# Causal blocks without the one above the diagonal: three columns of 64 queries per head in place of four, 64x64 products, a second load of x

## The reference, cut to what matters

```
q = layernorm(x);  k = v = ctx
ig, fg = gates(q, k, v)                       # one value per head and row
cs = cumsum(log_sigmoid(fg))
log_D = where(t <= s, cs[s] - cs[t], -inf) + ig[t]
D = exp(log_D - max over t);  C = (q k^T / 8) * D
h = C / (max(|sum C|, exp(-max)) + eps) @ v;  per-head layernorm * out_w
x = x + h;  x = x + fp8_gemm(layernorm(x)) + bias
```

## Time and profile before

| | us |
|---|---|
| median of 3 runs | 2239.78 (2235.75 to 2244.46) |
| the profiled execution | 2241.11 |
| its span, first to last instruction | 2239.0 |
| TensorE busy | 2020.9 (90%) |
| VectorE busy | 1865.2 (83%) |
| ScalarE busy | 1464.7 (65%) |
| GpSimd busy | 818.4 (37%) |
| mean granted clock of TensorE, as a share of full speed | 0.962 |

### The profile page before, as it was taken

One profiled execution on the slowest core, in us unless ns is written; L12 is line 12 of the kernel. 1 busy time (PEld: TensorE's weight loads), 2 busy tenths in 40 slices (PEclk: granted clock), 3 DMA queues, 4 the chain that ended last, 5 costly groups with the idle time before them and its releaser, 6 DMA issues. The chain is left out here.

```text
span 2239.0 us, 70236 instructions
## 1 busy us (share of the span) xinstructions
PE 2020.9 (90%) x26252; PEld 1445.6 (65%) x26252; DVE 1865.2 (83%) x4380; ACT 1464.7 (65%) x3137; POOL 818.4 (37%) x659
## 2 busy tenths in 40 slices
PE   2899999989999899998989999899998999989986
PEld 1666666666666666676666666666666766766763
DVE  5699987979889797897989979798887988979986
ACT  2677776757667576675767767576675766757753
POOL 0234343424334333433433433343343333434343
PEclk9999998989999999999999999999999999999998
DMA  5133323322323232232223233234232332332311
GB/s 164 23 112 94 108 94 96 98 87 87 114 87 103 71 115 87 87 114 87 87 88 114 87 101 101 87 86 115 87 97 77 115 87 87 114 87 87 105 39 38
DMA packets 206898, 207.82 MB, mean 93 GB/s; under 512 B 8848, under 2 KB 140816, under 8 KB 206496
## 3 DMA queue, kind: packets, MB, share of 16 engines
q1 hardware_dynamic: 206496, 202.59, 29.9%
HBM read 135.45 MB, written 67.11 MB: 90 GB/s over the span
## 5 line engine op out<-in xcount | busy, mean ns | idle before, releaser
L1082 POOL TENSOR_TENSOR x<-x,w_out 128x512 f32<-128x512 f32 x256 | 369.8, 1465 | 1078.3 <-DVE x L884 1078.3
L820 DVE TENSOR_TENSOR dec<-qk,dec 128x1024 f32<-128x1024 f32 x256 | 312.9, 1222 | 139.8 <-PE qk L420 88.5
L555 ACT ACTIVATE dec<-arg 128x512 f32<-128x512 f32 x512 | 301.3, 588 | 158.4 <-PE arg L406 158.3
L420 PE MATMUL qk<-qT,kT 64*128 64x128 f32 x4096 | 304.7, 290 | 71.4 <-issue 39.7
L1086 POOL TENSOR_TENSOR x<-x,x_sb 128x512 f32<-128x512 f32 x256 | 321.5, 1277 | 0.0
L420 PEld LDWEIGHTS qk<-qT,kT 64*128 64x128 f32 x4096 | 260.1, 195 | 85.9 <-issue 41.6
L445 PE MATMUL work<-c_sb,dec 128*64 128x65 f32 x8192 | 307.6, 230 | 1.3 <-DVE carry L828 1.3
L669 ACT ACTIVATE zq<-y,s_inv 128x1024 fp8e4<-128x1024 bf16 x128 | 142.5, 1114 | 229.3 <-PE y L466 229.3
L445 PEld LDWEIGHTS work<-c_sb,dec 128*64 128x64 f32 x8192 | 272.9, 143 | 29.1 <-issue 2.7
L481 PE MATMUL y<-w_ffn,zq 128*128 128x512 bf16 x1024 | 276.6, 394 | 0.0
L1074 POOL TENSOR_TENSOR k_w<-c_sb,facs 128x512 f32<-128x512 f32 x128 | 133.9, 1046 | 326.5 <-ACT facs L621 325.1
(11 more groups left out here) (108 smaller groups left out, 3362.4 us busy)
## 6 DMA issues: line engine op xcount, KB each, us to landing
x_sb<-in_x SPq DMA_DIRECT2D x128, 512.0 KB, 4.1
c_sb<-in_ctx SPq DMA_DIRECT2D x256, 256.0 KB, 5.4
out<-o_sb SPq DMA_DIRECT2D x128, 512.0 KB, 5.1
w_ffn<-in_L_ffn_kernel SPq DMA_DIRECT2D x1, 512.0 KB
w_out<-in_L_xattn_out_w SPq DMA_DIRECT2D x1, 256.0 KB
gsel<-in_c_gsel SPq DMA_DIRECT2D x1, 128.0 KB
b_ffn<-in_L_ffn_bias SPq DMA_DIRECT2D x1, 128.0 KB
ident<-in_c_ident SPq DMA_DIRECT2D x1, 64.0 KB
```

Source lines behind the costliest of these rows:

```text
L420: last = mm(qk_ps[:, u, c * P:(c + 1) * P], kT[half, r, c, t * P:(t + 1) * P], qT[half, r, c, t * P:(t + 1) * P], start=True, stop=True)
L555: af(dec[:, q, :], arg_ps, ACT.Exp).then_inc(decays[q].sem, 1)
L820: tt(dec[:, U * t:U * t + U, :], qk_ps[:, :, :], dec[:, U * t:U * t + U, :], ALU.mult).then_inc(weighted[t].sem, 1)
L1082: pl.tensor_tensor(h, h, w_out[:, :], ALU.mult).then_inc(h_scaled[t].sem, 1)
```

## The change

**The blocks.** Of a tile's 128x128 block of a head, the quarter with late keys and early queries is above the diagonal. The change works in quarters of 64x64. The lower half of the partitions (0 to 63) holds the first 64 keys of a tile, the upper half the last 64, and a head's three columns of 64 queries hold, for both tiles: the first keys of tile 0 by its first and second queries and the first keys of tile 1 by the second queries; above them the last keys in the same way (tile 1's keys stand with their halves exchanged). A head now takes 192 columns for both tiles in place of 256. `scores(b, p)` makes a pair of head pairs for both tiles, and `within` sums the first keys with `c_first`, a copy of the first 64 rows of each tile that is loaded extra, and the last ones with `c_sb`.

**TensorE.** `scores` goes from 8 products of 128x128 per call to 16 of 64 keys by 128 or 64 queries; `across` from 8 products of 128 queries to 16 of 64; `arg` from 6 matmuls over 512 or 128 columns to 14 over 256, 128 or 64 columns with 64 output partitions each; `scan_rows` from 4 to 16 on four column strips. Where a matmul reads 64 partitions and writes 64, it uses a quarter of the array.

**x and the output.** `x_sb` shrinks to 4 batches; x is loaded a second time for the residual, into `o_sb` itself (now two buffers), where `finish` later writes the output. So that load must wait for the store of two batches before.

**The order.** All five `slot` functions are written anew. Decays are double-buffered.

```diff
             def load_x(b):
-                r = b.k % RING
-                if b.follows(RING):
-                    sp.wait_ge(*x1_set[1].of(b - RING))
+                r = b.k % X_RING
+                if b.follows(X_RING):
+                    sp.wait_ge(*q_normed.of(b - X_RING))
                 sp.dma_start(x_sb[:, r, :, :], rows_of(x, b)).then_inc(x_in[r], 16)
+
+            def load_own(b):
+                if b.follows(2):
+                    sp.wait_ge(stored, b.count(16, -16))
+                sp.dma_start(o_sb[:, b.k % 2, :, :], rows_of(x, b)).then_inc(own_in[b.k % 2], 16)
...
+            def load_first(b):
+                r = b.k % 2
+                if b.follows(2):
+                    sp.wait_ge(*summed[1].of(b - 2))
...
             def arg(b, q):
...
-                mm(arg_ps, ident_bf[:, :], later[:, :].unsqueeze(1).broadcast_to([P, 4, P]),
-                   start=True, stop=False)
-                mm(arg_ps, tops[:, t * P:(t + 1) * P], hsel[:, row:row + NH - 1:2].unsqueeze(2).broadcast_to([P, 4, P]),
-                   start=False, stop=False)
-                for h in range(4):
...
+                mm(low[:, :, 0:2, :], tops[:, 0:Q], two, start=True, stop=False)
+                mm(high[:, :, 0::2, :], tops[:, 2 * Q:3 * Q], two, start=True, stop=False)
+                mm(low[:, :, 2, :], tops[:, 3 * Q:4 * Q], one, start=False, stop=False)
+                mm(high[:, :, 1, :], tops[:, Q:2 * Q], one, start=False, stop=False)
+                for h in range(2):
+                    neg = hsel_neg[:, row + U * h:row + U * h + 1].broadcast_to([P, Q])
+                    mm(low[:, h, 0:2, :], neg, tops[:, S:S + 2 * Q], start=False, stop=False)
+                    mm(high[:, h, 0::2, :], neg, tops[:, S + 2 * Q:S + 4 * Q], start=False, stop=False)
+                    mm(low[:, h, 2, :], neg, tops[:, S + 3 * Q:S + 4 * Q], start=False, stop=False)
+                    mm(high[:, h, 1, :], neg, tops[:, S + Q:S + 2 * Q], start=False, stop=False)
...
+                for i in range(2):
+                    c = 2 * p + i
+                    out = qk_ps[:, :, i * HEAD:(i + 1) * HEAD].rearrange("p u (s n) -> p u s n", s=3)
+                    for lower, key, query, n, to in ((True, 0, 0, 2, slice(0, 2)), (False, 3, 2, 2, slice(0, 3, 2)),
+                                                     (True, 2, 3, 1, slice(2, 3)), (False, 1, 1, 1, slice(1, 2))):
+                        for u in range(U):
...
             def across(b):
...
+                    for rows in (slice(0, P // 2), slice(P // 2, P)):
+                        for u in range(U):
...
-                if b.follows(1):
-                    act.wait_ge(*summed[q // U].of(b - 1))
-                af(dec[:, q, :], arg_ps, ACT.Exp).then_inc(decays[q].sem, 1)
+                if b.follows(2):
+                    act.wait_ge(*summed[1].of(b - 2))
+                af(dec[:, b.k % 2, q, :], arg_ps[:, 0:U * HEAD], ACT.Exp).then_inc(decays[q].sem, 1)
...
+                tt(mine, qk_ps[:, :, 0:U * HEAD], mine, ALU.mult).then_inc(weighted[p].sem, 1)
...
-                if t == 0 and b.follows(1):
-                    dve.wait_ge(stored, b.count(16, 0))
...
             def residual(b, t):
                 pool.wait_ge(*h_scaled[t].of(b))
-                pl.tensor_tensor(x1[:, b.k % 2, t, :], x1[:, b.k % 2, t, :], x_sb[:, b.k % RING, t, :],
+                if t == 0:
+                    pool.wait_ge(own_in[b.k % 2], b.count(16, 16, 2))
+                pl.tensor_tensor(x1[:, b.k % 2, t, :], x1[:, b.k % 2, t, :], o_sb[:, b.k % 2, t, :],
```

More of the change, by code:

```diff
@@ L316, in slot @@
             def slot(m):
[L317 to L322, removed]
+                if live(m + 5):
+                    load_c(m + 5)
+                if live(m - 3):
+                    load_own(m - 3)
+                if live(m - 2):
+                    load_first(m - 2)
+                if live(m - 4):
+                    store(m - 4)
+                if live(m + 7):
+                    load_x(m + 7)
             slots(sp, slot)
@@ L435, in within @@
             def within(b, t):
-                pe.wait_ge(*weighted[t].of(b))
+                r = b.k % RING
+                for p in range(2):
+                    pe.wait_ge(*weighted[p].of(b))
                 if t:
@@ L440, in within @@
                     pe.wait_ge(*state_kept.of(b))
+                    pe.wait_ge(first_in[b.k % 2], b.count(32, 32, 2))
                 for u in range(U):
[L442 to L447, removed]
+                    for c in range(C):
+                        at = c % 2 * HEAD
+                        heads_dec = dec[:, b.k % 2, c // 2 * U + u, at:at + HEAD]
+                        cols = slice(u * W, (u + 1) * W)
+                        for rows, slot, src in ((slice(0, Q), 0, c_first[:, b.k % 2, t, c, cols]),
+                                                (slice(Q, P), 1 + t, c_sb[:, r, t, c, cols])):
+                            last = mm(work_ps[rows, u, c * W:(c + 1) * W], heads_dec[:, slot * Q:(slot + 1) * Q], src,
+                                      start=True, stop=True)
                 last.then_inc(summed[t].sem, 1)
@@ L452, in across @@
                 pe.wait_ge(*state_kept.of(b))
+                pe.sem_inc(pe_passed, 1)
                 for c in range(C):
[L454 to L457, removed]
+                    for rows in (slice(0, P // 2), slice(P // 2, P)):
+                        for u in range(U):
+                            half = slice(DH * u, DH * u + DH)
+                            last = mm(work_ps[rows, u, c * W:(c + 1) * W],
+                                      qT[half, b.k % RING, c, P + rows.start:P + rows.stop],
+                                      state[half, c, :], start=True, stop=True)
                 last.then_inc(crossed.sem, 1)
@@ L741, in _ @@
             setup(ve.memset(n_eps[:, :], EPS))
+            for t in range(T):
+                for r in range(2):
+                    setup(ve.memset(c_first[t * Q:(t + 1) * Q, r, t, :, 0:U * W:U * W - 1], 1.0))
             setup(ve.memset(ln_qs[:, :], math.log(Q_SCALE)))
```

360 lines of the change are left out of this document (190 added, 170 removed).

## The result

The changed kernel takes 2402.62 us (median of 4 runs, 2387.95 to 2405.53) against 2238.33 (2235.75 to 2244.46) for the one before in the same comparison: ratio 1.0713, 95% interval 1.0688 to 1.0738. It is slower by 7%; 2117 was forecast, with a range of 2010 to 2225.

The account below looks back on a forecast made before the run. The DMA loop was to replace TensorE as bound: 86.4 + 5 of filling and setup, 127 plain slots at 13.7, 31 scan extras at 5.0, 14 loop starts at 7.5 and 25.3 give 2116.6, forecast 2117; range 2010 to 2225.

Parts of the forecast that it names:

- What bounds the kernel: Before the change, TensorE bounds a plain slot at 14.41; scans add 5.35 per four slots, a loop start 9.5.
- TensorE and VectorE, part by part: Plain slot after the change: TensorE falls from 14.41 to 13.1, VectorE from 12.74 to 12.2.
- The new loop through the DMA queue: From store through own load, residual, statistics and finish to the next store: 13.7 a plain slot, replacing TensorE as bound.
- Own lands 8.7 after the store's issue (8.3 to 9.1): In the DMA loop, the second load of x lands 8.7 after the issue of the store in that slot.
- The clock: Rival: TensorE idling in scan slots lowers its clock; scans cost 8 and loop starts 14, 2301 in all; 5 in 100.
- 8.7 + 1.4 + 3.4 + 0.2 = 13.7: DMA loop in a plain slot: own's landing, residual with handover, VectorE to the end of finish, then the store's issue.
- Where the loop starts again: At each restart of the eight-slot loop, TensorE's and VectorE's standings overlap: 7.5 instead of 9.5, between 6 and 10.
- The DMA loop is late: Rival: five transfers a slot in one queue make a plain slot 14.3, 2193 in all; 20 in 100.
- own landing more than 10 behind the store: Sign in the DMA loop that would show the forecast wrong: own landing more than 10 after the store's issue.

Follow-up runs that it names:

- the fast version: Changed kernel with the second load of x in its own buffer one slot earlier and the first rows of ctx one slot earlier: 2078.71 us, ratio 0.9278.
- The changed order: Changed kernel with the second load of x and the first rows of ctx issued ahead of ctx's three pieces in SyncE's slot: 2202.79 us, ratio 0.9832.
- The table of four kernels: Changed kernel 2402.62 us; first rows of ctx a slot earlier 2362.25; own buffer for the second x, a slot earlier, 2341.12; both 2078.71.

## Why the prediction was wrong

**What bounds the kernel.** Right once the new waits are gone. The fast version is the forecast without them: forecast 13.1 for TensorE, 5.0 for the scans, 7.5 a start; measured 13.23, 5.8 (17.60 + 14.62 - 2 x 13.23, for undisturbed slots), and, from its first `keep_heads` at 90.7 to its last at 2044.5, (1953.8 - 127 x 13.23 - 31 x 5.8) / 14 = 6.7. The scans lie above their range of 4.5 to 5.35. The 25.3 behind the last `keep_heads` in the sum is 1.0 more than its rows give (24.3), which changes nothing.

**TensorE and VectorE, part by part.** Right within 0.1 a term: the quadrants run four at once, a change of shape costs 0.12 to 0.15, the score product 0.952. The Trainium skill (TensorEngine Tiling, Key Properties) says that a change of the tiling mode drains TensorE, and these rows agree that it costs something; that did not help, since the bound had left TensorE.

**The step that failed is "The new loop through the DMA queue": "Own lands 8.7 after the store's issue (8.3 to 9.1)".** In batches 16 to 111 it landed 10.9 behind it in the median, 9.3 to 11.4 in the middle 8 of 10. My 8.7 was a piece of ctx of before, issued 2.0 behind the first transfer and landing 5.4 later, plus 1.3 for 512 KB. Own was issued 3.8 behind the store, not 2.0, and took 7.0 from there, not 6.7: the issue is the term that I had too small. Two things hold it. Four issues (x and three pieces of ctx) stand between the store's and that of own, and the store must have landed, which takes 3.3; I had named this wait and given it no time. The changed order tells them apart. There own is issued 3.2 behind the store, 0.02 after the store's landing, and takes 5.6 to its own, which gives 8.9. So of the 2.0 gained the issues ahead of own are 0.6 and the transfers of ctx ahead of it 1.4; the wait for the store stays. With 10.9 for 8.7 the sum comes to 15.9 of the 17.0 measured.

**The second loop had no price.** "The extra load of ctx's first rows queues behind own and is needed by the first `within` at about the same time" was one sentence, where it was a loop of its own: `load_first` waits for `summed[1]` of two batches before and is issued last of all behind the store; it landed 11.8 behind it in the slot shown. From there `within`, scores, `across` and `carried` lead to `finish` and the next store. The table of four kernels shows that it alone holds the kernel at 2341.

**The clock.** The forecast had the idle only in the scan slots. In the changed kernel TensorE now waits for `c_first` in 107 of the 128 batches, and behind the wait of 2.62 in the slot shown the granted clock was that of the lower level, 1.2 GHz. Windows of the changed kernel, the wait, what follows, and then:

```profile
1203.20:1206.60 3.40, 0.78 (x9) 0.53 (x8) 0.66 (x2) 0.00 (x0) 0.81 (x1) 0.98 0.54 91
1206.60:1210.00 3.40, 3.40 (x80) 3.28 (x84) 2.15 (x7) 1.49 (x4) 2.68 (x3) 0.52 0.00 0
1210.00:1213.00 3.00, 2.97 (x83) 2.54 (x74) 2.51 (x8) 1.98 (x5) 0.00 (x0) 1.00 0.04 8
```

`within` and scores took 1.93 + 1.34 where 1.08 + 0.86 would do, 1.3 more. Not every wait costs clock as well: behind that of 2.74 in the next slot the clock stayed at its upper level. Of the 101 waits for `c_first` that were longer than 0.5, 42 had a mean clock under 0.75 in the microsecond behind them and 52 the upper level. With two levels a mean clock of 0.900 means 0.2 x 2404 = 481 us at the lower one, against 0.076 x 2239 = 170 before. In the kernel with the earlier first rows that wait is gone, TensorE waits for `carried` instead (241.6), and the mean clock is still 0.903. Forecast 8.7 + 1.4 + 3.4 + 0.2 = 13.7 became 11.1 + 1.4 + 4.8 + 0.2 = 17.5 in that slot. In the 4.8 lie VectorE's wait of 1.04 for TensorE and the shift of a later x (line 886, 0.45), both outside my 3.4.

**Where the loop starts again.** The sum was nearly right and the reason half right: the standings overlap as I said, and are twice as long, because they now fall among the loads and the instructions' packets wait behind these.

**The rivals.** "The DMA loop is late" was the right one, and I capped it at 14.3 a plain slot, 2193. I had written that own landing more than 10 behind the store would make the forecast wrong; it should have been a case of the sum and not a remark behind it.

## What to carry to other kernels

A load whose buffer is freed by a store closes a loop through the queue. Price it as the later of two times, the store's landing and the issues ahead of the load, plus all transfers under way, plus everything in the strict order up to the next store, and compare with the slot; do so for every load that is issued behind that store, since two such loops side by side hide each other, and removing one of them shows little (40 or 61 of 324 here). A buffer of its own for one load and one slot of lead for both turned 2403 into 2079 here, with the same number of bytes.

Where a loop starts again its engines stand. Here starts moved apart cost 72, 53 and 30, starts without loads gave 32, and half as many starts gave 35. So try a longer loop first, and keep the starts together.

## What the runs showed of the hardware

- An engine's standing at the start of a loop depends on what the DMA engines carry then: TensorE 3.4 to 3.8 with no loads, 5.1 to 7.3 among them, VectorE 2.8 to 3.0 against 5.6 to 6.0. The Trainium skill (Runtime: NRT & Kernel Launch, Instruction fetch mechanics) says that a taken branch to a page that is not at hand has the page fetched by a DMA before the engine goes on. The trace agrees: a 16 KB packet of the instruction queue starts 1.0 behind TensorE's branch without loads and 3.2 in the fast version, takes about 1.0, and TensorE goes on 1.5 later.
- A body twice as long does not make a start dearer: TensorE stood 5.3 to 5.7, against 5.1 to 7.3.
- 64 MB more of loads, last in the queue of the kernel before, cost nothing (ratio 0.9988).
- Four products on the four quarters of the array run at once: `across` on quarters takes 0.62 to the next row, as 8 products of 128 queries 1.04.
